# Last pass of a four-layer spectral network: eight transposes in one block over two banks, the inverse y transform once per half step

## The reference, cut to what matters

```python
# 64 images of 64 x 64 pixels; 32 channels; 4 layers; 12 x 12 modes at both ends of x
h = layer_norm(x @ fc0_w + fc0_b, ln0_g, ln0_b)
for i in range(4):
    x_ft = rfft2(h)                               # only 24 x 12 modes are kept
    out_ft = einsum('bixy,ioxy->boxy', x_ft[modes], w1[i] or w2[i])
    h = irfft2(out_ft) + einsum('bchw,oc->bohw', h, conv_w[i]) + conv_b[i]
    h = layer_norm(h, ln_g[i], ln_b[i])
    if i < 3: h = gelu(h)
h = gelu(h @ fc1_w + fc1_b)                       # 32 -> 128
h = gelu(h @ fc2_w + fc2_b)                       # 128 -> 64
h = h @ fc3_w + fc3_b                             # 64 -> 1, one number per pixel
# then: text tokens are joined on, a local attention and an expert network follow
```

## Time and profile before

| | us |
|---|---|
| time, median of 3 runs (lowest, highest) | 3235.67 (3233.77, 3237.13) |
| span of the profiled execution | 3238.3 |
| PE busy (matmul) | 2941.1 (91%) |
| DVE busy | 2306.9 (71%) |
| ACT busy | 2158.6 (67%) |
| POOL busy | 2115.6 (65%) |
| last pass, first `i1_last` to last `out_copy` | 1829.4 to 2645.1 |

### The profile page before, as it was taken

One profiled execution on the slowest core, in us unless ns is written; L12 is line 12 of the kernel. 1 busy time (PEld: TensorE's weight loads), 2 busy tenths in 40 slices (PEclk: granted clock), 3 DMA queues, 4 the chain that ended last, 5 costly groups with the idle time before them and its releaser, 6 DMA issues. The chain is left out here.

```text
span 3238.3 us, 190683 instructions
## 1 busy us (share of the span) xinstructions
PE 2941.1 (91%) x80542; PEld 1998.9 (62%) x80542; DVE 2306.9 (71%) x3829; ACT 2158.6 (67%) x3644; POOL 2115.6 (65%) x1147
## 2 busy tenths in 40 slices
PE   6877999997999998799999689999999969999998
PEld 4555777775777776577777434444444426777776
DVE  7766888984889886588888344444444428999996
ACT  5664777774677775477777267777777755655654
POOL 3763999993899995599999234444444425666663
PEclk9997999999999999899999789999999988999998
DMA  5764555554455554455554411111111110000000
GB/s 167 222 220 155 174 177 175 173 184 134 153 175 175 181 174 162 125 176 178 177 171 163 134 49 56 58 58 55 57 59 60 48 49 12 14 13 13 13 13 10
DMA packets 215406, 369.21 MB, mean 114 GB/s; under 512 B 116051, under 2 KB 133267, under 8 KB 215011
## 3 DMA queue, kind: packets, MB, share of 16 engines
q1 hardware_dynamic: 203602, 353.37, 34.2%
q10 hardware_dynamic: 7920, 10.03, 1.0%
q0 software_dynamic: 3744, 3.84, 0.8%
HBM read 209.43 MB, written 157.71 MB: 113 GB/s over the span
## 5 line engine op out<-in xcount | busy, mean ns | idle before, releaser
L1481 POOL TENSOR_TENSOR rstd<-var,mhalf 128x16 f32<-128x16 f32 x512 | 1524.3, 2993 | 689.2 <-DVE var L1238 683.7
L1238 DVE TENSOR_REDUCE var<-sq 128x16 f32<-128x528 f32 x384 | 403.5, 1052 | 87.9 <-ACT sq L903 87.3
L1252 DVE TENSOR_TENSOR zt<-ps,rstd 128x512 f32<-128x512 f32 x512 | 345.4, 684 | 77.9 <-POOL rstd L1481 71.8
L615 PEld LDWEIGHTS ps<-d,hp 128*32 128x32 f32 x24576 | 292.6, 111 | 132.0 <-ACT hp L915 98.5
L615 PE MATMUL ps<-d,hp 128*32 128x48 f32 x24576 | 345.6, 209 | 27.0 <-ACT hp L915 16.6
L544 PEld LDWEIGHTS ps<-cwl,hc 64*64 64x64 f32 x16384 | 272.8, 139 | 138.9 <-issue 132.7
L527 PE MATMUL ps<-zb,ex 48*128 48x512 f32 x1024 | 301.0, 664 | 55.8 <-DVE zt L1252 20.5
L555 PEld LDWEIGHTS ps<-dyi,gt 64*48 64x48 f32 x16384 | 230.1, 124 | 160.3 <-issue 148.7
L1074 ACT ACTIVATE a<-ps,fc1b 128x1024 f32<-128x1024 f32 x256 | 271.3, 1111 | 64.7 <-PE ps L818 64.7
L544 PE MATMUL ps<-cwl,hc 64*64 64x64 f32 x16384 | 308.5, 226 | 0.0
L903 ACT ACTIVATE sq<-ps 128x512 f32<-128x512 f32 x384 | 218.9, 598 | 129.5 <-PE ps L544 118.4
(11 more groups left out here) (198 smaller groups left out, 4999.7 us busy)
## 6 DMA issues: line engine op xcount, KB each, us to landing
h_scratch<-ho SPq DMA_DIRECT2D x256, 512.0 KB
hc<-h_scratch SPq DMA_DIRECT2D x256, 512.0 KB, 3.9
wsb<-in_w SPq DMA_DIRECT2D x64, 288.0 KB
gin<-g_scratch SPq DMA_DIRECT2D x252, 72.0 KB
gin<-g_scratch SPq DMA_DIRECT2D x504, 36.0 KB
g_scratch<-hp ACTq DMA_DIRECT2D x32, 192.0 KB, 4.8
g_scratch<-hp SPq DMA_DIRECT2D x32, 192.0 KB, 3.9
tokens<-wsb SPq DMA_DIRECT2D x256, 4.0 KB
```

The source lines that it names most:

```text
L615: last = nc.tensor.matmul(a_ps[row:row + 32, 2 * TRIG * k:2 * TRIG * k + 2 * TRIG], hp[b][:, u, 8 * j + k].rearrange("p v r -> p (v r)"), ...
L1238: nc.vector.tensor_reduce(dst, src, axis=AX.X, op=ALU.add).then_inc(var_ready, 1)
L1252: nc.vector.tensor_tensor(by_px(zt[h][:, u]), by_px(main_ps(s, h, u)), scale, ALU.mult).then_inc(norm_ready, 1)
L1481: nc.gpsimd.tensor_tensor(rstd[u][:], var[u][:], mhalf[:], ALU.pow).then_inc(rstd_ready, 1)
```

## The change

In the last pass alone:

- `turn_last` issues a half step's eight transposes in one block, four into bank 2 and four into bank 3, with one wait at its head (all `affine` of the half step before, and the `out_copy` that read bank 3), and a signal after each four. It stands behind the first half's `fc2_rows`.
- ACT does both `affine` right behind the first half's second GELU.
- `fc3_rows`, which writes bank 3 too, waits for both `affine` of this half step (`turned_before`).
- `i1_last` does all eight channels of a half step at once, into 256 columns of banks 6 and 7, as the last part of PE's half step; `z_copy_last` copies 112x256 twice instead of 112x128 four times, at the end of DVE's half step. The counts of `zl_ready` are halved.

```diff
-        t_mid, t_last = ps[:, 4, :], ps[:, 2, :]
-        z_mid, z_last = [ps[:, 5 + c, :] for c in range(2)], [ps[:, 6 + c, 0:128] for c in range(2)]
+        t_mid, t_last = ps[:, 4, :], [ps[:, 2 + k, :] for k in range(2)]
+        z_mid, z_last = [ps[:, 5 + c, :] for c in range(2)], [ps[:, 6 + c, 0:256] for c in range(2)]
...
-            def i1_last(b, g, h, e):
+            def i1_last(b, g, h):
...
-                    at_least(pe, zl_ready, 8 * g + 4 * h + 2 * e)
+                    at_least(pe, zl_ready, 4 * g + 2 * h)
                 waits_apart(pe, passed)
-                for k in range(4):
-                    last = modes(z_last, b, 8 * h + 4 * e + k, k)
+                for k in range(8):
+                    last = modes(z_last, b, 8 * h + k, k)
...
-            def turn_last(g, h, k, first, end):
+            def turn_last(g, h):
                 n = 4 * rank(LAYERS, g) + 2 * h
                 pe.wait_ge(norm_ready, n + 2)
-                pe.wait_ge(hc_ready, n + k)
-                for a in range(first, end):
-                    src = zt[h][:].rearrange("p u (n r) -> p (u n) r", r=8)[:, :, 2 * a + k]
-                    last = nc.tensor.transpose(t_last[:, 128 * a:128 * a + 128], src, ident[:])
-                if end == 4:
+                pe.wait_ge(hc_ready, n)
+                at_least(pe, hst_ready, 2 * g + h - 2)
+                waits_apart(pe, passed)
+                for k in range(2):
+                    for a in range(4):
+                        src = zt[h][:].rearrange("p u (n r) -> p (u n) r", r=8)[:, :, 2 * a + k]
+                        last = nc.tensor.transpose(t_last[k][:, 128 * a:128 * a + 128], src, ident[:])
                     last.then_inc(t_ready, 1)
...
+            def turned_before(g, h):
+                n = 4 * g + 2 * h + 6
+                return 4 * PAIRS * LAYERS + (min(n, 4 * PAIRS) if isinstance(n, int) else n)
...
                 pe.wait_ge(a2_ready, 8 * g + 4 * h + 4)
+                pe.wait_ge(hc_ready, turned_before(g, h))
                 at_least(pe, hst_ready, 2 * g + h)
+                waits_apart(pe, passed)
...
-                        if k == 1 and c:
-                            turn_last(*c, k, 0, 2)
                         if heads:
                             fc2_rows(*heads, k)
-                        if nxt:
-                            i1_last(1 - p, *nxt, k)
-                        if c:
-                            turn_last(*c, k, 2 * k, 4)
+                        if k == 0 and c:
+                            turn_last(*c)
+                        if k == 1 and nxt:
+                            i1_last(1 - p, *nxt)
...
-                        if c:
-                            affine(*c, k)
+                        if k == 0 and c:
+                            affine(*c, 0)
+                            affine(*c, 1)
...
-            def z_copy_last(b, g, h, e):
-                dve.wait_ge(zl_psr, 4 * g + 2 * h + e + 1)
+            def z_copy_last(b, g, h):
+                dve.wait_ge(zl_psr, 2 * g + h + 1)
                 for c in range(2):
-                    nc.vector.tensor_copy(z_part_last(zb[b], CH * c + 8 * h + 4 * e, 4),
-                                          z_last[c][0:64 + 2 * TRIG].rearrange("k (c n r) -> k c n r", c=4, r=8)
+                    nc.vector.tensor_copy(z_part_last(zb[b], CH * c + 8 * h, 8),
+                                          z_last[c][0:64 + 2 * TRIG].rearrange("k (c n r) -> k c n r", c=8, r=8)
...
                     if behind(i, p, h, 0, 2):
                         reduce(s, 2 * i + p, h, 0)
-                    if nxt:
-                        z_copy_last(1 - p, *nxt, 0)
...
-                        z_copy_last(1 - p, *nxt, 1)
+                        z_copy_last(1 - p, *nxt)
```

More of the change, by code:

```diff
@@ L520, in widen @@
                     if is_last(s):
-                        pe.wait_ge(zl_ready, 8 * g + 8)
+                        pe.wait_ge(zl_ready, 4 * g + 4)
                     else:
@@ L570, in i1 @@
                     last.then_inc(z_psr, 1)
-            def i1_last(b, g, h, e):
-                if h == 0 and e == 0:
+            def i1_last(b, g, h):
+                if h == 0:
                     pe.wait_ge(gt_ready, rank(LAYERS, g) - PAIRS + 1)
                 if isinstance(g, int):
-                    at_least(pe, zl_ready, 8 * g + 4 * h + 2 * e)
+                    at_least(pe, zl_ready, 4 * g + 2 * h)
                 waits_apart(pe, passed)
-                for k in range(4):
-                    last = modes(z_last, b, 8 * h + 4 * e + k, k)
+                for k in range(8):
+                    last = modes(z_last, b, 8 * h + k, k)
                 last.then_inc(zl_psr, 1)
@@ L814, in fc1_rows @@
                 at_least(pe, a2_ready, 2 * n)
-                pe.wait_ge(zl_ready, batches_before(g, h, k))
+                pe.wait_ge(zl_ready, batches_before(g, h))
                 for y in range(4):
@@ L821, in fc1_rows, with batches_before @@
                 last.then_inc(f1_psr, 1)
-            def batches_before(g, h, k):
-                n = 8 * g + 4 * h + 2 * k + 16
-                return min(n, 8 * PAIRS) if isinstance(n, int) else n
+            def batches_before(g, h):
+                n = 4 * g + 2 * h + 8
+                return min(n, 4 * PAIRS) if isinstance(n, int) else n
+            def turned_before(g, h):
+                n = 4 * g + 2 * h + 6
+                return 4 * PAIRS * LAYERS + (min(n, 4 * PAIRS) if isinstance(n, int) else n)
             def fc2_rows(g, h, k):
@@ L883, in _ @@
             for h in range(2):
-                for e in range(2):
-                    i1_last(0, 0, h, e)
-            pe.wait_ge(zl_ready, 8)
+                i1_last(0, 0, h)
+            pe.wait_ge(zl_ready, 4)
             last_pass(LAYERS)
@@ L938, in affine @@
                 act.wait_ge(t_ready, 4 * rank(LAYERS, g) + 2 * h + k + 1)
-                nc.scalar.activation(ho[h][:, 4 * k:4 * k + 4].rearrange("p a n -> p (a n)"), t_last, ACT.Identity,
+                nc.scalar.activation(ho[h][:, 4 * k:4 * k + 4].rearrange("p a n -> p (a n)"), t_last[k], ACT.Identity,
                                      bias=lnp[:, 1:2], scale=lnp[:, 0:1]).then_inc(hc_ready, 1)
@@ L1465, in _ @@
             for h in range(2):
-                for e in range(2):
-                    z_copy_last(0, 0, h, e)
+                z_copy_last(0, 0, h)
             coefficients(1, 1)
```

## The result

The changed kernel takes 3267.3 us (median of 4 runs, 3264.0 to 3271.6) against 3234.9 for the kernel before in the same comparison: the ratio is 1.0097, with a 95% interval of 1.0083 to 1.0112, so it is 27 to 36 us slower. The span of the profiled execution is 3264.0 us against 3238.3.

What follows compares the result with a forecast made beforehand. PE's queue was taken to bound the kernel before, a chain through three engines the changed one. 60 x 0.55 = +33.0, -1.1 ahead of the loop, +0.5 drain: +32.4 on the 3238.3 span, median 3268 us, range 3240 to 3288.

Steps and rivals of the forecast that it cites:

- The chain: Whole half step: a chain through PE, ACT and DVE, ending in i1_last, copies, normalise, closes the loop; +0.55 us each.
- The chain through ACT: Second half: ACT's GELU paces it, so all PE sheds there brings 0.11 us; fc3_rows waits to about 6.33 at no cost.
- The rest of the sum: Last pass: 60 half steps at +0.55 us give +33.0; ahead of the loop -1.1, drain +0.5; sum +32.4 us.
- the rival of a PE bound: Last pass: PE's queue stays the bound, half step 11.7 instead of 12.04 us, 3214 us in all; chance 0.13.
- So the queue of PE sets the pace of this pass now.: Last pass before the change: PE, busy 116.58 of 120 us, was taken to pace the half step of 12.04 us.
- They are PE work that covers DVE's copies.: Old order: four transposes between each inverse y transform and the fc1_rows waiting for its copies were said to cover them.
- the case where both cancel: Half step: i1_last 0.5 us earlier through a shorter GELU chain on ACT, -0.1 to +0.1 us, 3229 to 3242; chance 0.10.
- The fall of the clock: PE's waits lower its clock, about 2.7 us a fall: +162 us in every half step, 3295 in one of six; chance 0.04.

Runs made afterwards that it cites:

- e2: Kernel before with only the inverse y transform done once per half step and its copies merged, transposes unchanged: ratio 1.0048, half step 12.30 us.
- e3: Changed kernel with one of the two copies of a half step given to ACT: ratio to the kernel before 1.0034, half step 12.29 us.
- e4: Changed kernel with the first normalise of each half step ahead of the copies in DVE's queue: ratio to the kernel before 1.0055, half step 12.37 us.
- e1: Kernel before with only the block of eight transposes, both affine behind it and the new fc3 wait: ratio 1.0064, half step 12.49 us.
- e9: Changed kernel with one spare matmul of 256 columns behind the inverse y transform: ratio to the kernel before 1.0079, half step 12.54 us.
- e6: Kernel before with only the first normalise of each half step moved ahead of DVE's second pair of copies: ratio 0.9942, half step 11.82 us.
- e8: Kernel before with the last two transposes of each half step done four times over (six more): ratio 1.0025, half step 12.24 us.

## Why the prediction was right, and where a step of it wasn't

Predicted were 3268 us and slower; measured are 3267.3. The comparison by steps, in us from the start of `widen`:

| step | predicted | changed kernel |
|---|---|---|
| block of transposes starts | 4.01 | 4.02 |
| both `affine` over | 6.26 | 6.22 |
| `fc1_rows`, second half | 5.08 | 5.11 |
| first GELU, second half | 6.29 | 6.32 |
| wait of `fc3_rows` | about 0.2 | 0.20 |
| `i1_last` starts | 9.47 | 9.50 |
| copies over | 11.31 | 11.25 |
| PE idle ahead of `fc1_rows` | 0.88 | 0.88 |
| `normalise` over | 12.50 | 12.44 |
| half step | 12.6 | 12.50 here, 12.54 on average |

- **The chain** held in every row, and it is what costs: its arithmetic gives 9.47 us to the transform and a longer way from there to `widen`, and 9.50, 1.80 and 1.24 were measured. e2, e3 and e4 show that the way behind the transform is paid (longer transform and copies, copies side by side, `normalise` early), e1 that the way ahead of it is, and e9 that PE's own work in the wait is not. The single most useful number was the duration of a copy that no trace showed: 0.417 by the slope between 128 and 512 columns, 0.416 measured.
- **The chain through ACT** held to 0.03 us: shedding PE work in the second half brought 0.1 us only, as the GELU paces it. `fc3_rows` started at 6.46, not 6.33; it cost nothing, since the half steps without its wait have their transform at 9.50 as well.
- **The rest of the sum** was slightly high: +0.48 us a half step on average instead of +0.55. Three half steps of four went from 11.95 or 12.04 to 12.49 or 12.58, +0.54, as forecast. The fourth took 12.28 already before, with a pause of DVE that the rows of one half step don't show, and went to 12.57, +0.29. Inside the half step the transform and DVE's start behind it took 0.99 and not 1.08. 60 x 0.48 is 29, with the 1.4 us gained ahead of the loop some 27 to 28 us, at the lower end of the measured 27 to 36. The hit to the microsecond is partly luck. (In the rival of a PE bound, 12.04 less 0.38 and 0.05 is 11.6, not 11.7; nothing else hangs on it.)
- **The step that failed** is in the first part: "So the queue of PE sets the pace of this pass now." It named as near misses what already closed the loop. e6 takes 0.23 us off a half step of the kernel before without touching PE's order, and e8 fills PE to 100% for a third to a half of what PE-bound work would cost. The kernel before was paced by a chain too: PE's queue from `widen` to the second half's `fc1_rows`, then the GELUs (4.39 us to the transform), then the copies, for which `fc1_rows` waited 0.19 us, and then `normalise`, which stood behind the second copies in DVE's queue. The forecast came out right all the same because the half step was worked out as a chain, not as PE's sum.
- **A second reading that failed** is beside it: "They are PE work that covers DVE's copies." The two transposes behind the last transform covered nothing that was paid (1.17 us with them, 1.18 in e1 without). What the block costs is its place: four more transposes ahead of the second half's `fc1_rows`, +0.43 in e1. The sum didn't use this reading; it counted the block where it stands, with the 1.07 us ahead of `fc1_rows`.
- **The rivals.** PE-bound (3214 us) and the case where both cancel (3229 to 3242) are refuted by the time itself, and e9 shows why the first fails: its reading of the 97% was wrong, as above. The fall of the clock did not come in the middle of the pass: 1.00 at PE waits of 0.88 us.
  In the half steps with text work the granted clock falls as before (0.76 and 0.78 from 1900 to 1920 and 1920 to 1940 us, against 0.84 and 0.76), and one of them took 18.26 us against 16.30. No cost of the change can be read there: the first eight half steps took 117.8 us in the changed kernel and 114.1 in e9, whose later ones are as long.
  The Trainium skill (TensorE: Matmul & The Clock Gate, "PE-mode transpose") has it that transposes don't count as PE activity for the clock gate in the way that matmuls do. Whether that is so stays open here: with eight in a block and 0.88 us of waiting in each 12.5 the granted clock stayed at 1.00.
- The Trainium skill (Perfetto Trace Analysis, "Optimizing Scalar/DVE Operations") says that where Vector isn't saturated but causes bubbles on other engines, breaking instructions up may allow work to be completed sooner. The trace agrees: DVE had 2.16 us of idle time ahead of the copies, so saving it instructions gained nothing, and joining them with their transforms (e2) made the way to `fc1_rows` 0.63 us longer.

## What to carry to other kernels

Before work is gathered into a block, ask in whose way the block will stand. Transposes that lay in a wait cost nothing; moved ahead of the matmul on which the longest chain hangs, they cost their full time (e1, 0.43 us for four), though PE does the same work. Joining two pieces into one at the end of the chain puts the first piece's time on the chain as well (e2: 0.63 us more behind the transform, against 0.32 less ahead of it). A busy share of 97% doesn't prove that an engine paces, and an idle time on it doesn't measure a loss (in e1 the wait behind the transform grew from 0.19 to 0.61 us, and `fc1_rows` came no later behind the transform): lay out one period, and compare how far apart its stations lie before and after. Look at each of the periods that the loop is written out for, since one of them may be longer. And where a copy and an independent operation share a queue, put the one whose input is there first ahead; here that alone was worth 0.6% (e6).

## What the runs showed of the hardware that I had not expected

- DVE pauses 0.16 to 0.23 us ahead of `normalise` in one half step of four, which the trace puts down to "issue" (0.23 in e3's rows above). That is once per turn of the loop, which is written out for four half steps. Before, it made each fourth half step 12.28 us instead of 11.95 or 12.04. In the changed kernel it is gone (12.57 to 12.60 beside 12.58), in e3, with one short copy in place of two, it is back. In the kernel before, e1, e3, e6 and e8 `normalise` starts 0.64 to 0.66 us behind the start of the copies in that half step, whether these take 0.49 or 0.42; where they take 0.76 on DVE (e2 and the changed kernel) it starts 0.67 to 0.69 behind in every half step. This fits something that runs beside the copies for some 0.65 us; that it is the loop's branch is argued, not shown.
- Three fp32 matmuls of 256 columns with the same 128x128 weights took 1.49 us, 0.25 for each of the six instructions that they become; a further transpose of 128 columns, one instruction, costs 0.11.
